# Where the norm statistics of the last keys are made in the first cross-attention

## The reference, cut to what matters

```
mu, var = mean(x, -1), var(x, -1)
xn  = (x - mu) * rsqrt(var + 1e-5) * gamma_x + beta_x        # x: the 12,544 keys
k_x = rope_rotate_k((xn @ Wkv)[..., :512]);  v_x = (xn @ Wkv)[..., 512:]
sim = (q * 64 ** -0.5) @ concat(k_x, k_l).T                  # 8 heads of 64, softmax over all keys
out = softmax(sim) @ concat(v_x, v_l) @ Wo
```

## Time and profile before

| | us |
|---|---|
| runs of the kernel before, median of 3 | 2481.84 (2480.80 to 2481.87) |
| the profiled execution, own time | 2482.87 |
| its span | 2481.1 |
| busy in the span: PE | 2228.8 (90%) |
| busy: DVE, ACT, POOL | 1826.3 (74%), 1185.9 (48%), 519.5 (21%) |
| busy share of the 16 DMA engines by q1 (SP's queue) | 55.4% |

### The profile page before, as it was taken

How to read it: one execution, slowest core, us unless ns; L and a number is a source line. 1 busy time by engine, 2 the same in 40 slices (tenths; PEclk the granted TensorE clock), 3 DMA queues, 4 the chain that set the end, 5 groups by cost and what they waited for, 6 DMA issues and landing times. The chain is left out here.

```text
span 2481.1 us, 56935 instructions
## 1 busy us (share of the span) xinstructions
PE 2228.8 (90%) x21794; PEld 1434.9 (58%) x21794; DVE 1826.3 (74%) x2833; ACT 1185.9 (48%) x2053; POOL 519.5 (21%) x300
## 2 busy tenths in 40 slices
PE   2999979999996969999988899999997559999979
PEld 1444436666665836666667555566655415555548
DVE  6788878999996267777734688888886877777721
ACT  4566653344444337888763333323232416565542
POOL 0555540000000030000001166655552010000000
PEclk7999999999997969999998999999998759999989
DMA  8577765676655567878745322222211347677654
GB/s 285 204 243 242 237 222 142 193 208 188 175 176 196 190 151 186 183 181 184 177 105 193 122 104 71 85 104 104 104 60 51 106 110 172 158 167 165 154 149 171
DMA packets 245977, 398.00 MB, mean 160 GB/s; under 512 B 28921, under 2 KB 210304, under 8 KB 245668
## 3 DMA queue, kind: packets, MB, share of 16 engines
q1 hardware_dynamic: 240132, 393.90, 55.4%
q10 hardware_dynamic: 5664, 1.44, 0.3%
HBM read 316.44 MB, written 78.06 MB: 159 GB/s over the span
## 5 line engine op out<-in xcount | busy, mean ns | idle before, releaser
L1631 DVE CUSTOM_DVE_ANT_0 l3x_junk<-l3x_pm,l3x_mrow,l3x_top 128x896 bf16<-128x896 f32 x224 | 247.0, 1148 | 73.3 <-PE l3x_pm L1787 68.3
L1715 ACT ACTIVATE l1x_prob<-l1x_ring,mask_col 128x512 f32<-128x512 f32 x392 | 248.2, 685 | 81.5 <-PE l1x_ring L1807 80.0
L1718 ACT ACTIVATE l3x_prob<-l3x_ring 128x512 f32<-128x512 f32 x392 | 204.6, 601 | 154.1 <-PE l3x_ring L1811 152.8
L2800 POOL TENSOR_TENSOR l2x_gk<-l2x_f,first_vin 128x1024 f32<-128x1024 f32 x98 | 184.3, 1917 | 161.1 <-DVEq L2541 161.1
L1174 ACT ACTIVATE l0x_att_pt<-l0x_att_pt 128x1024 f32<-128x1024 f32 x99 | 104.7, 1058 | 167.4 <-DVE l0x_att_pt L1115 163.9
L1207 PE MATMUL l0x_att_pv<-l0x_wv,l0x_att_vin 128*128 128x512 f32 x392 | 181.9, 607 | 0.0
L2674 PE MATMUL l2x_kf<-l2w_w,l2x_nin 128*128 128x512 f32 x392 | 173.4, 602 | 4.5 <-DVE l2x_f L2515 4.5
L2674 PE MATMUL l2x_kf<-l2w_w,l2w_first 128*128 128x512 f32 x392 | 170.2, 594 | 0.0
L2515 DVE SCALAR_TENSOR_TENSOR l2x_f<-l2x_kf,l2x_rs,l2w_bias 128x1024 f32<-128x1024 f32 x98 | 125.8, 1284 | 55.6 <-PE l2x_kf L2674 42.7
L1631 DVE CUSTOM_DVE_ANT_0 l1x_junk<-l1x_pm,l1x_mrow,l1x_top 128x896 bf16<-128x896 f32 x112 | 123.6, 1148 | 43.8 <-PE l1x_pm L1787 43.8
L1811 PE MATMUL l3x_ring<-l3x_ident,l3x_mtile 128*128 128x512 bf16 x392 | 151.4, 386 | 0.0
(11 more groups left out here) (737 smaller groups left out, 4950.6 us busy)
## 6 DMA issues: line engine op xcount, KB each, us to landing
first_kt<-scratch_KS SPq DMA_DIRECT2D x84, 448.0 KB, 9.1
scratch_KT<-l0x_max_kf SPq DMA_DIRECT2D x28, 896.0 KB, 4.7
l0x_att_kt<-scratch_KT SPq DMA_DIRECT2D x56, 448.0 KB, 7.1
scratch_KS<-l0x_side_kp SPq DMA_DIRECT2D x14, 1344.0 KB, 13.4
l1x_kt<-scratch_KS SPq DMA_DIRECT2D x42, 448.0 KB, 9.4
scratch_KS<-first_kt SPq DMA_DIRECT2D x14, 1344.0 KB, 5.9
l3x_kt<-scratch_KS SPq DMA_DIRECT2D x42, 448.0 KB, 8.9
l0fw_w<-L_ffn_exp_w SPq DMA_DIRECT2D x16, 1024.0 KB, 7.8
```

The source lines that it names most:

```text
L1631: dve.tensor_tensor_reduce(junk[x % 2][:, :, :], pm[x % 2][:, :, 0:SPLIT], mrow[b][:, :].rearrange("p (s k) -> p s k", s=2), 1.0, top[1 - ...
L1715: ins = act.activation(into, scores, ACT.Exp, bias=R.mask_col[:, bass.ds(m * TILES + n // 4, 1)])
L1718: ins = act.activation(into, scores, ACT.Exp)
L2800: pool.tensor_tensor(gk[b][:, t, :, 0:HD], f[b][:, t, :].rearrange("p (h d) -> p h d", h=H), ks[b][:, 2, t, :].unsqueeze(2).broadcast_to([ ...
```

## The change

The opening makes the statistics of chunks 0 to 9 only (`pieces` and `parts` have one entry, all loops end at `keys.EARLY`, one turn, copy and store). The last 28 tiles go to a new class `LateStats`. In the pass ScalarE loads them by its own queue, two tiles at a time (256 KB) into two buffers, and makes their squares in 14 steps, one behind each call of `both` in the first seven bodies, which are now written out. VectorE makes the variance behind body 6 and the reciprocal behind body 7; ScalarE makes the root and stores the 28 columns straight to the row in DRAM. SP waits for that store before it loads the factors of the chunks from 20 on.

```
+class LateStats:
+    TILES, AT_ONCE, STEPS = 4 * TILES, 2, 7
+    def load(self, act, k):
+        if k >= 2:
+            act.wait_ge(self.sem("squared"), k - 1)
+        act.dma_start(self.raw[k % 2][:, :, :], self.src[self.first // self.AT_ONCE + k]).then_inc(
+            self.sem(f"raw{k % 2}"), 16)
+    def squares_about_mean(self, act, k):
+        ...
+        act.wait_ge(self.sem(f"raw{b}"), 16 * (k // 2 + 1))
+        if k:
+            act.wait_ge(self.sem("squared"), k)
+        for t in range(self.AT_ONCE):
+            last = act.activation(self.junk[t][:, :], self.raw[b][:, t, :], ACT.Identity,
+                                  accum_out=self.total[:, first + t:first + t + 1])
+        last.then_inc(self.sem("totals"), 1)
+        ...
+        act.activation(self.minus[:, both], self.total[:, both], ACT.Copy, scale=-1.0 / DIM)...
+        for t in range(self.AT_ONCE):
+            last = act.activation(self.junk[t][:, :], self.raw[b][:, t, :], ACT.Square,
+                                  bias=self.minus[...], accum_out=self.spread[...])
+        last.then_inc(self.sem("squared"), 1)
+    def variance(self, dve):
+        dve.wait_ge(self.sem("squared"), 2 * self.STEPS)
+        dve.tensor_scalar(self.spread[:, :], self.spread[:, :], 1.0 / DIM, EPS, ALU.mult, ALU.add)...
+    def root(self, act): ...        # waits for variance; Sqrt
+    def reciprocal(self, dve): ...  # waits for root; into R.rs[:, columns]
+    def store(self, act):
+        act.wait_ge(self.sem("columns"), 1)
+        act.dma_start(self.R.rs_row.rearrange("o (t p) -> p (o t)", p=P)[:, self.columns], self.R.rs[:, self.columns],
+                      allow_slow_non_contiguous=True).then_inc(self.sem("stored"), 16)
 ...
 # SP, in the pass
-                sp.wait_ge(S.sem("stats_stored1"), 16)
                 ahead = 2
-                with sp.Fori(0, steps - 1 - ahead) as i:
+                known = late.first * P // MAX_CHUNK // 2 - 1
+                with sp.Fori(0, known) as i:
+                    for b in range(2):
+                        load_next(b, i)
+                        spill(b, i)
+                sp.wait_ge(S.sem("late_stored"), 16)
+                with sp.Fori(known, steps - 1 - ahead) as i:
 ...
 # VectorE, in the pass
-                with dve.Fori(0, steps - 1) as i:
-                    both((1, i), (0, i), (0, i + 1))
-                    both((0, i + 1), (1, i), (1, i + 1))
+                for first, stop, step in ((0, late.STEPS, late.variance), (late.STEPS, late.STEPS + 1, late.reciprocal),
+                                          (late.STEPS + 1, steps - 1, None)):
+                    with dve.Fori(first, stop) as i:
+                        both((1, i), (0, i), (0, i + 1))
+                        both((0, i + 1), (1, i), (1, i + 1))
+                    if step:
+                        step(dve)
 ...
 # ScalarE, in the pass
-                run_ahead(act, steps, prepare, both, copy_all)
+                late.load(act, 0)
+                late.load(act, 1)
+                prepare(0, 0)
+                for i in range(late.STEPS):
+                    for ahead, now in (((1, i), (0, i)), ((0, i + 1), (1, i))):
+                        both(ahead, now)
+                        k = 2 * i + now[0]
+                        late.squares_about_mean(act, k)
+                        if k + 2 < 2 * late.STEPS:
+                            late.load(act, k + 2)
+                late.root(act)
+                both((1, late.STEPS), (0, late.STEPS))
+                both((0, late.STEPS + 1), (1, late.STEPS))
+                late.store(act)
+                with act.Fori(late.STEPS + 1, steps - 1) as i:
+                    both((1, i), (0, i))
+                    both((0, i + 1), (1, i))
+                both((1, steps - 1), (0, steps - 1))
+                copy_all(1, steps - 1)
 ...
 # the opening: SP, ScalarE, VectorE, TensorE
-                    for m in range(keys.DEPTH, M):
+                    for m in range(keys.DEPTH, keys.EARLY):
-                    keys.store(sp, 1)
-                        if m == keys.EARLY:
-                            keys.root(act, 0)
-                    keys.root(act, 1)
+                    keys.root(act, 0)
-                    keys.variance(dve, key_link, 1)
-                    keys.reciprocal(dve, 1)
-                    keys.copy(dve, 1)
+                    keys.variance(dve, key_link, 0)
+                    keys.reciprocal(dve, 0)
+                    keys.copy(dve, 0)
```

More of the change, by code:

```diff
@@ L483, in __init__ @@
         n, early = R.keys // P, self.EARLY * TILES
-        self.pieces = [slice(0, early), slice(early, n)]
-        self.parts = [((0, self.SCALAR_FROM), (self.SCALAR_FROM, self.EARLY)), ((self.EARLY, self.M),)]
+        self.pieces = [slice(0, early)]
+        self.parts = [((0, self.SCALAR_FROM), (self.SCALAR_FROM, self.EARLY))]
         self.raw = [sb(f"raw{b}", [P, TILES, DIM]) for b in range(self.DEPTH)]
@@ L576, in store, with __init__, sb, sem @@
             self.sem(f"stored{k}"), 16)
+class LateStats:
+    TILES, AT_ONCE, STEPS = 4 * TILES, 2, 7
+    def __init__(self, nc, S, A, R, mem):
+        def sb(name, shape, dt=F32):
+            return mem.enter_context(nc.sbuf_tensor(f"{S.name}_late_{name}", shape, dt))
+        self.S, self.R = S, R
+        self.first = R.keys // P - self.TILES
+        self.columns = slice(self.first, self.first + self.TILES)
+        self.src = A["ctx"].rearrange("(n t p) d -> n p t d", t=self.AT_ONCE, p=P)
+        self.raw = [sb(f"raw{b}", [P, self.AT_ONCE, DIM]) for b in range(2)]
+        self.junk = [sb(f"junk{t}", [P, DIM]) for t in range(self.AT_ONCE)]
+        self.total, self.minus, self.spread = [sb(n, [P, self.TILES]) for n in ("total", "minus", "spread")]
+    def sem(self, n):
+        return self.S.sem("late_" + n)
+    def load(self, act, k):
[4 more added lines that the diff above has]
+    def squares_about_mean(self, act, k):
+        b, first = k % 2, k * self.AT_ONCE
+        both = slice(first, first + self.AT_ONCE)
+        act.wait_ge(self.sem(f"raw{b}"), 16 * (k // 2 + 1))
[5 more added lines that the diff above has]
+        last.then_inc(self.sem("totals"), 1)
+        act.wait_ge(self.sem("totals"), k + 1)
+        act.activation(self.minus[:, both], self.total[:, both], ACT.Copy, scale=-1.0 / DIM).then_inc(self.sem("minus"), 1)
+        act.wait_ge(self.sem("minus"), k + 1)
+        for t in range(self.AT_ONCE):
+            last = act.activation(self.junk[t][:, :], self.raw[b][:, t, :], ACT.Square,
+                                  bias=self.minus[:, first + t:first + t + 1],
+                                  accum_out=self.spread[:, first + t:first + t + 1])
+        last.then_inc(self.sem("squared"), 1)
+    def variance(self, dve):
+        dve.wait_ge(self.sem("squared"), 2 * self.STEPS)
+        dve.tensor_scalar(self.spread[:, :], self.spread[:, :], 1.0 / DIM, EPS, ALU.mult, ALU.add).then_inc(
+            self.sem("variance"), 1)
+    def root(self, act):
+        act.wait_ge(self.sem("variance"), 1)
+        act.activation(self.minus[:, :], self.spread[:, :], ACT.Sqrt).then_inc(self.sem("root"), 1)
+    def reciprocal(self, dve):
+        dve.wait_ge(self.sem("root"), 1)
+        dve.reciprocal(self.R.rs[:, self.columns], self.minus[:, :]).then_inc(self.sem("columns"), 1)
+    def store(self, act):
+        act.wait_ge(self.sem("columns"), 1)
+        act.dma_start(self.R.rs_row.rearrange("o (t p) -> p (o t)", p=P)[:, self.columns], self.R.rs[:, self.columns],
+                      allow_slow_non_contiguous=True).then_inc(self.sem("stored"), 16)
@@ L587, in __init__ @@
         self.raw = [S.sb(f"max_raw{b}", [P, DC, MAX_CHUNK]) for b in range(2)]
-        self.rows = [S.sb(f"stats_rows{k}", [P, P]) for k in range(2)]
+        self.rows = [S.sb("stats_rows", [P, P])]
         self.rs = [S.sb(f"max_rs{b}", [P, MAX_CHUNK]) for b in range(2)]
@@ L636, in rotated_keys @@
         psc = ps("ps", HEADS)
+        late = LateStats(nc, S, A, R, mem)
         sem = lambda n: S.counted("max_" + n)
@@ L2128, in l0_xattn @@
             keys = KeyStats(nc, S, A, R, mem, pass_loads.rows)
-            M = keys.M
             mask = sb("mask", [R.keys // P, P])
@@ L2186, in _ @@
                     act.activation(bias_v[:, :], pbv[:, :], ACT.Copy).then_inc(S.sem("banks_read"), 1)
-                    for m in range(keys.SCALAR_FROM + 2, M):
+                    for m in range(keys.SCALAR_FROM + 2, keys.EARLY):
                         keys.squares_about_mean(act, m)
-                        if m == keys.EARLY:
-                            keys.root(act, 0)
-                    keys.root(act, 1)
+                    keys.root(act, 0)
                 @block.vector
@@ L2197, in _ @@
                     norm_vector(dve, link, S, "m", xn[:, :], ln[:, :], nw2)
-                    for m in range(M):
+                    for m in range(keys.EARLY):
                         keys.stats(dve, m)
@@ L2275, in _ @@
```

(3 more changed lines are left out.)

## The result

| | before | after |
|---|---|---|
| runs side by side, median of 4 each | 2481.86 (2480.80 to 2482.03) | 2509.79 (2508.04 to 2512.66) |
| the profiled execution, own time | 2482.87 | 2508.49 |
| its span | 2481.1 | 2506.7 |

The ratio is 1.0108 (95% interval 1.0096 to 1.0120). By the medians the changed kernel is 27.9 us slower. The forecast was 2502, its range 2486 to 2524. The page's totals of the changed kernel hardly tell a story: the work has moved, none has grown much. Columns: busy us (share of the span) and instructions of each engine.

A forecast was written before the change was run, and what follows sets the result against it. A closed loop of 10.39 us per chunk through ScalarE, VectorE and GpSimd, tied to a full TensorE, was taken as the bound. Terms -8.9 + 23.8 + 3.2 + 2.0 = +20.1 us gave 2502, range 2486 to 2524.

The forecast's parts named there:

- opening: Before the pass: four chunks fewer let the pass start at 52.0 instead of 60.92, -8.9 us.
- steps: Fourteen on ScalarE behind the second half's rounding, inside the loop: 2.83 us each, period 12.15 instead of 10.39, +23.8 us.
- variance, root, reciprocal: In the pass: VectorE waits for the fourteenth squares with fold, rotation and scaling queued behind, +3.2 us.
- store by ScalarE: In the pass: issuing 3,584 pieces of 4 bytes holds ScalarE for 3.5 us, less 1.2 of slack, +2 us.
- Idle time hides the steps (1): In the pass: copies can be late without cost by the whole 2.83, leaving only the opening: 2474; chance 9%.
- The rhythm isn't regained (2): In the pass after the steps: 11.1 us a chunk for some 12 chunks, 8 us more: 2510; chance 14%.
- The fold stays at 2.02 (3): VectorE's fold in the pass stays slow in its new place, +13 us: 2515; chance 7%.
- ScalarE blocked by the store (4): In the pass: the store blocks ScalarE for most of 22.5 us, +19: 2521; chance 9%.
- The clock falls in the steps (5): TensorE's clock falls in gaps of 1.7 us a chunk in the pass, +70 us: 2570; chance 3%.
- The opening isn't shorter (6): Before the pass: an unseen cause limits the gain to 4.5 us: 2506; inside the forecast's own range, no separate chance.

The follow-up runs named there:

- kernel 1: The changed kernel without the fourteen steps of squares and their loads in the pass, variance taken of a constant: 2483.99, ratio 1.0000 to the kernel before.
- kernel 2: The changed kernel with squares and loads moved into ScalarE's idle time before the rounding of the second half: 2484.49, ratio 1.0004 to the kernel before.
- kernel 5: The kernel before plus one ScalarE copy of 1.0 us per chunk behind the rounding of the second half: 2487.95, ratio 1.0015.
- kernel 6: The kernel before plus one ScalarE copy of 2.0 us per chunk behind the rounding of the second half: 2507.22, ratio 1.0095.
- kernel 7: The kernel before plus one ScalarE copy of 2.0 us per chunk in the idle time ahead of the second half's rounding: 2484.55, ratio 1.0003.
- kernel 3: The changed kernel with VectorE's variance half a body (one chunk) later and the root behind it: 2502.24, ratio 1.0070 to the kernel before.
- kernel 4: The changed kernel with the late factors turned by VectorE and stored as 112 runs of 128 bytes in four DMAs: 2501.59, ratio 1.0071.
- kernel 8: The changed kernel with squares in the idle time, loads one step ahead, variance later and store in runs: 2474.70, ratio 0.9963 to the kernel before.

## Why the prediction was right, point by point

The side and the range held; the time came out 7.8 us over the forecast of 2502. Of these, 5.5 lie between the profiled executions (2508.49 against 2503.0). The other 2.3 come from the medians: before it lay 1.0 under its profiled execution, now 1.3 over it. The steps' mechanism was right. The largest term wrong was the store, whose mechanism was another, and errors of both signs partly cancelled.

| step | forecast | measured (profiled executions) |
|---|---|---|
| opening | -8.9 | -10.2 at the first rounding, -9.7 at the start of the pass |
| steps | +23.8 | +20.1 (intervals 1 to 14) |
| variance, root, reciprocal | +3.2 | +6.9 (intervals 15 to 17, with step 14 in them) |
| store by ScalarE | +2.0 | +9.0 (intervals 18 to 27) |
| sum | +20.1 | +25.8 |

*The steps.* The mechanism held (kernels 1, 2 and 5 to 7): idle time in one place isn't room in another. The step was taken as 2.83 (measured 2.76), the period as 12.15 (12.03), the slack as 1.2 (1.1), the fold as 1.08 (1.09). The Trainium skill (SBUF — State Buffer, Who interferes with whom) describes the lock behind this slack. The traces agree: the fold beside an addition ended 0.96 us after it in the kernel before and 0.95 in kernel 5. The sizes were less good. By kernel 3 the steps cost 21.4 where 23.8 was forecast: 1.64 each with a load and not 1.76, and 1.0 for the thirteenth, without a load, and not 1.3. The 0.2 of that step in the table holds the 0.8 by which the waiting variance shortened its interval. Steps and variance together were forecast as 27.0 and came as 27.0: the steps were put too high and the variance too low by as much, which was luck.

*The variance.* VectorE was held as forecast, with fold, rotation and scaling behind it. What I left out is the TensorE: it waits for that rotation, which frees the bank, stands for 3.73 us, and starts again at a granted clock of 0.50. The term was 3.2 against 6.9 in the table, or 5.6 with kernel 3 as the measure. An estimate of the clock's share is 1.5 us, the two waits of VectorE for the slow matmuls (0.36 + 1.17); no run changed the clock alone.

*The store* was the mis-sized term, 2.0 against 9.0, and its mechanism was another one. I priced the time for which ScalarE issues (3.5, less the slack), and listed as a rival that it would be blocked for longer. The issue took 0.42. A line beside those of the earlier trace rows spoke against so high a bound: ScalarE issued another column of 256 pieces (l0x_gx, at 5.12) in 0.59 us, where the one I used took 1.61. The price lay in the transfers: the pieces held up those beside them, and their buffers came free late, as kernel 4 shows. I had called SP's wait for the landing free. It stood there for 6.6 us, though its next load had to wait longer for something else (281.42). And I asked nothing about the spills. That the forecast's range still took this in is due to its upper bounds, which were set for other reasons. The rule cited from the Trainium skill (DMA: Bandwidth & Descriptors, Rules for kernel authors), one descriptor per element, agrees: q10 carried 3,600 packets. No price stands there; the runs give one.

*The rivals.* Idle time hides the steps (1): false where they were put, true in the gap (kernels 2 and 7). The rhythm isn't regained (2): false, four intervals of 10.38 to 10.40 follow each other in kernel 4 behind the store; that its 2510 is the number measured (2509.79) is chance. The fold stays at 2.02 (3): false, 1.09. ScalarE blocked by the store (4): false as put, 0.42 us of ScalarE. Its 2521 lies 11 from the result, the forecast 8; the store was the costly part it named, by another way. The clock falls in the steps (5): false, 1.00. The opening isn't shorter (6): false.

*Left open*: the clock's share of the variance stall beyond the estimate; most of the 3.7 us of kernel 5; and the chunk of 17.0 us near the end of the pass (interval 23), which stands in the kernel before as well and which no run here was made for.

## What to carry to other kernels

Idle time of an engine can only be used where it lies in the loop: 2.76 us of work cost 1.64 a chunk behind the rounding and nothing ahead of it. Look for the instruction that the waiting one holds, and for what lies queued behind it; an accidental overlap such as the slow fold tells how much slack there is. And price a DMA by its pieces and by what is in flight beside it, not by its bytes or by the time of its issue.

## What the runs showed of the hardware that I had not expected

A store of 14 KB in 3,584 pieces of 4 bytes was issued in 0.42 us and landed after 18.2 (19.0, 22.8 and 18.4 in kernels 1 to 3). Beside it spills of 896 KB landed after 13.5 us instead of 4.5, and of 448 KB after 15.0 instead of 5.0, through a queue of another engine. The pass paid about 9 us (8.3 between the profiled executions of the change and kernel 4); the same factors in 112 runs of 128 bytes cost 1.3 (the one interval of 11.7 in kernel 8).
